# Counting sort of a GNN kernel: counts on two engines, one scan for the first columns, reload in two parts

## The chip, the cores and the metric

The kernel runs on one core of a Trainium2 chip. The metric is the device time of one execution in microseconds (us). "Before" is the kernel as it stood, "after" the kernel with the change below. Engines are called by their names in the profile: PE (TensorE), DVE (VectorE), ACT (ScalarE), POOL (GpSimd), SP (SyncE).

## What is computed

Four graph networks in a row work on 3125 nodes of 128 features and 50,000 edges. Each needs gathers by source node and sums by destination node. The first of them is, in short:

```python
h = jnp.maximum(_layernorm(x), 0.0)                   # 3125 x 128
h = relu(_bn(h @ fc_w + fc_b))
for i in range(2):
    d = segment_sum(ones, col)                        # degrees
    val = edge_weight * rsqrt(d[col]) * rsqrt(d[row])
    z = segment_sum(val[:, None] * h[row], col) @ conv_w[i] + conv_b[i]
    h = relu(_bn(z)) + h
x = x + h
```

The three others (an attention over `leaky(h_src, h_tgt, edge features)`, a dot-product attention with 8 heads, and two gated sums) go over the same edges. Per edge, `edge_attr @ W_edge @ a` is wanted too (4 scores).

## The kernel before

**Stages.** The nodes are split into NB = 25 blocks of 128. The edges are first sorted by destination block, so that each tile of 128 edges belongs to one block; there are TILES = 416 tiles with padding, in GROUPS = 52 groups of G = 8 tiles. Then six passes run over the tiles (`PASSES`), one for each layer. In each of them POOL issues one indirect DMA for each tile (L568, 416 a pass), which gathers 128 rows of a table in DRAM; DVE builds one-hot matrices, PE sums by them. Between two passes the node features go through PE, ACT and DVE, and SP stores the next table (`tab_dram[k]`, L498 and L500).

**The sort.** The edges lie as 125 lanes by COLS = 400 columns. SP loads `e_dst`, `e_src`, `e_w` (L470 to L472, semaphore `s_load_e`), then `wedge`, the small `abd` columns, the first two parts of the edge features (`ea`), `x`, and writes the initial records `recS` to `rec_dram` (L487, semaphore `s_recinit`). DVE makes constants (L1240 to L1252), fills `recS` and `rec_all` (L1254 to L1260), works out the block `e_blk` of each edge (L1265, L1266), local numbers, the record's fields (L1268 to L1273), counts for each lane and each of the 25 blocks how many edges lie in it (L1279, `tot`), and waits for two matmuls on PE (`prefixes`, L958) that turn the counts into bases. PE reaches `prefixes` in its edge-feature loop when i is 2 (L996). Eight small instructions (L1286 to L1293) make `base_pos`. `place(0, FIRST, ...)` then gives the first 80 columns their places: for each of 25 blocks a comparison (L1302), a scan (L1305) and a predicated copy (L1310), and five instructions that turn places into row numbers (L1315 to L1319). `place(FIRST, COLS, ...)` does the other 320.

**Scatter and reload.** POOL waits for the initial records (`s_recinit`) and for the first places (`s_placed`), then writes the records of one column after the other with 400 indirect DMAs (L545); group g of 8 columns also waits for the edge scores of ACT (`s_esc`). It needs the second `s_placed` at column 80. When all have landed, SP loads the sorted records back into `recU` (L491), and after that it stores the table of pass 0, which has been ready for long. DVE copies the source numbers out of `recU` (L1628), and POOL's first gather waits for that and for the stored table. While POOL gathers, DVE clears `ACC` (L1633), makes the first one-hots (L1624) and splits the records into three bf16 parts (`split`, L1520 to L1523).

**Order.** Each engine runs its instructions in order of the program. `link` waits for the instruction before it, `queued` does not. SP's and ACT's DMAs are issued in order of their programs too. Nothing is planned by a scheduler.

Of the kernel before, what the change touches and what calls it, by code (L numbers as in the profile page):

```python
# [8 lines left out]
ALU = mybir.AluOpType  # L9
ACT = mybir.ActivationFunctionType  # L10
AX = mybir.AxisListType.X

P = 128
# [8 lines left out]
FIRST = 80  # L22
TILES = (E // P + NB + 15) // 16 * 16
# [107 lines left out]
def gnn_kernel(nc, x, src, dst, edge_attr, edge_weight, fc_w, fc_b, conv_w, conv_b, bn_gamma, bn_beta,  # L131
               W_node, W_edge, a_vec, Wq, bq, Wk, bk, Wv, bv, Wo, bo, Wt, bt, Wg, bg, out):
    ctx = ExitStack()
    with ctx:
# [13 lines left out]
        lane_i = sb("lane_i", [P, 1], I32)  # L148
        iota = sb("iota", [P, 512])
# [132 lines left out]
        ranks = OH[0:LANES, :, :, :].rearrange("p a t f -> p (a t f)")[:, 0:5 * COLS].rearrange("p (c e) -> p c e", e=COLS)  # L282
        newblk = sb("newblk", [P, 2, SLOTS * H + 1])
# [17 lines left out]
        s_tot = sem("s_tot")  # L301
        s_pre = sem("s_pre")
# [166 lines left out]
        def _(sp):  # L469
# [16 lines left out]
            sp.wait_ge(s_recdef, 1)  # L486
            sp.dma_start(rec_rows, recS[:, :, :].rearrange("p t r -> p (t r)")).then_inc(s_recinit, 16)  # L487

            for r in range(3):
                sp.wait_ge(s_scat[r], 16 * G * ((COLS // G - 1 - r) // 3 + 1))  # L490
            sp.dma_start(recU.rearrange("p t r -> p (t r)"), rec_rows).then_inc(s_recl, 16)  # L491
# [11 lines left out]
            for k in range(len(PASSES)):  # L503
# [70 lines left out]
        def _(act):  # L574
# [6 lines left out]
            for k, v in enumerate([fc_b, conv_b[0], conv_b[1], bn_gamma[0], bn_gamma[1], bn_gamma[2],  # L581
                                   bn_beta[0], bn_beta[1], bn_beta[2]]):
                act.dma_start(cols[:, k:k + 1], v.rearrange("(p o) -> p o", o=1)).then_inc(s_load_w, 16)
            for k, v in enumerate([bo, bt[0], bt[1], Wg[0], Wg[1]]):
                act.dma_start(cols[:, 9 + k:10 + k], v.rearrange("(p o) -> p o", o=1)).then_inc(s_load_w, 16)
            for k, v in enumerate([bq, bk, bv]):
                act.dma_start(bqkv[:, k, :], v.rearrange("(o f) -> o f", o=1).broadcast_to([P, D])).then_inc(s_load_w, 16)
            act.dma_start(bgb[:, :], bg.rearrange("(o f) -> o f", o=1).broadcast_to([P, 2])).then_inc(s_load_w, 16)
# [50 lines left out]
            def only(chunk, work):  # L639

                return lambda c, n: work() if c == chunk else None

# [215 lines left out]
        def _(pe):  # L858
# [109 lines left out]
            pe.wait_ge(s_ue, 1)  # L968

# [19 lines left out]
            for i, buf, loads in edge_loads(pe):  # L989
# [6 lines left out]
                if isinstance(i, int) and i == 2:  # L996
                    prefixes()
# [217 lines left out]
        def _(dve):  # L1215
# [24 lines left out]
            link(v.tensor_copy(iota[:, :], iota_i[:, :]))  # L1240
            link(v.tensor_copy(lane[:, :], lane_i[:, :]))
# [5 lines left out]
            link(v.memset(sg16[:, :, :, :], 0.0))  # L1247
            link(v.memset(zero, 0.0))
            link(v.memset(onesb[:, :], 1.0))
            link(v.memset(c128b[:, :], float(P)))  # L1250
            link(v.tensor_scalar(lane_diag[:, :, :], ident[:, :].unsqueeze(1).to_broadcast([P, 4, P]), lane[:, 0:1], None, ALU.mult))
            link(v.tensor_scalar(iota2[:, :], iota[:, 0:P], 2.0, -float(P - 1), ALU.mult, ALU.add))  # L1252
            dve.sem_inc(s_consts, 1)
            link(v.memset(recS[:, :, :], 0.0))  # L1254
            link(v.memset(recS[:, :, R_DST], float(P)))
            dve.sem_inc(s_recdef, 1)


            dve.wait_ge(s_load_e, 48)
            link(v.memset(rec_all[:, :, :], 0.0))  # L1260
            link(v.tensor_scalar(spare[:, :], lane[:, :], float(COLS), float(P * TILES - LANES * COLS), ALU.mult, ALU.add))
            link(v.tensor_scalar(row_all[:, :], iota[:, 0:COLS], spare[:, 0:1], None, ALU.add))
            dve.sem_inc(s_recbase, 1)
            for ends, blk, loc in ((e_dst, e_blk[:, :], rec[:, :, R_DST]), (e_src, e_sblk[:, :], e_sloc[:, :])):
                link(v.tensor_single_scalar(e_int[:, :], ends[:, :], 7, ALU.arith_shift_right))  # L1265
                link(v.tensor_copy(blk, e_int[:, :]))  # L1266
                link(v.tensor_copy(e_rank[:, :], ends[:, :]))
                link(v.scalar_tensor_tensor(loc, blk, -float(P), e_rank[:, :], ALU.mult, ALU.add))  # L1268
            link(v.tensor_copy(rec[:, :, R_SRC], e_rank[:, :]))
# [4 lines left out]

            scratch = [e_rank[:, :], e_pos[:, :]]
            with dve.Fori(0, NB // 5, 1) as b5:
                for c in range(5):
                    b = 5 * b5 + c
                    v.tensor_scalar(scratch[c % 2], e_blk[:, :], iota[0:LANES, bass.ds(b, 1)], 0.0, ALU.is_equal, ALU.add,  # L1279
                                    accum_out=tot[:, bass.ds(b, 1)]).then_inc(s_tot, 1)  # L1280
                    if c:
                        dve.wait_ge(s_tot, b)
                dve.wait_ge(s_tot, 5 * b5 + 5)
# [10 lines left out]
            link(v.memset(e_pos[:, :], 0.0))  # L1294
            link(v.memset(e_w[:, :], 0.0))

            def place(c0, c1, ranked, carry):

                step = 16 if carry else 15
                with dve.Fori(0, NB // 5, 1) as b5:  # L1300
                    for c in range(5):
                        v.tensor_scalar(inside[:, c, c0:c1], e_blk[:, c0:c1], iota[0:LANES, bass.ds(5 * b5 + c, 1)], None, ALU.is_equal).then_inc(s_rank, 1)  # L1302
                    for c in range(5):
                        dve.wait_ge(s_rank, ranked + step * b5 + c + 1)
                        v.tensor_tensor_scan(ranks[:, c, c0:c1], e_w[:, c0:c1], inside[:, c, c0:c1], base_pos[:, bass.ds(5 * b5 + c, 1)],  # L1305
                                             ALU.add, ALU.add).then_inc(s_rank, 1)
                    for c in range(5):
                        dve.wait_ge(s_rank, ranked + step * b5 + 10 + c)
                        dve.sem_inc(s_gate, 1)
                        v.copy_predicated(e_pos[:, c0:c1], inside[:, c, c0:c1], ranks[:, c, c0:c1]).then_inc(s_rank, 1)  # L1310
                    if carry:
                        v.tensor_copy(base_pos[:, bass.ds(5 * b5, 5)], ranks[:, :, c1 - 1]).then_inc(s_rank, 1)
                    dve.wait_ge(s_rank, ranked + step * b5 + step)
# [7 lines left out]

            place(0, FIRST, 0, True)
            place(FIRST, COLS, 16 * NB // 5, False)

# [289 lines left out]
            def sum_pass(k, weighted):  # L1614
# [11 lines left out]

                dve.wait_ge(s_recl, 16)
                link(v.tensor_copy(idx_u[:, :], recU[:, :, R_SRC]))  # L1628
# [380 lines left out]
```

## Time and profile before

| what | value |
|---|---|
| time, median of 3 runs | 4109.13 us (4102.37 to 4113.22) |
| the profiled execution: its time | 4107.58 us |
| the profiled execution: its span in the trace | 4105.7 us |
| POOL busy | 2773.8 us, 2902 instructions |
| DVE busy | 1833.0 us |
| PE busy | 1935.3 us |
| ACT busy | 1079.0 us |
| first scatter starts, last starts | 73.23 us, 585.78 us |
| first gather starts | 601.03 us |

The span is what the trace covers; the execution's time is 1.9 us longer. A row of a timeline gives the start, the duration, the engine, the line, what is written and read, and in brackets how long the engine was idle before and what released it. DMA_INDIRECT on POOL is the work of making the descriptors of one indirect DMA, not the transfer.

### The profile page before, as it was taken

The page shows a single profiled execution, that of the slowest core. Times are in us where ns is not written, and L with a number is a line of the kernel's source. Part 1 is how long each engine was busy: PE and PEld are TensorE (multiplying, and loading weights), DVE is VectorE, ACT ScalarE, POOL GpSimd, SP SyncE. Part 2 cuts the span into 40 slices and gives each one's busy share as a digit, 9 for nine tenths or more (in the row PEclk, how much of TensorE's full clock was granted, in tenths as well). Part 3 has the DMA queues.
Part 4 walks back from the last instruction along what each step waited for, and adds up shares of the span by engine and source line. Part 5 has one row for each costly group of instructions (what it writes and reads, how often), then busy time and mean ns, then how long its engine had stood idle before and what let it go on. Part 6 is the DMA issues. An engine that isn't in the chain of part 4 may idle for free. (4 is left out here: it accounts for less than half of the span.)

```text
span 4105.7 us, 45490 instructions
## 1 busy us (share of the span) xinstructions
PE 1935.3 (47%) x10431; PEld 1712.0 (42%) x10432; DVE 1833.0 (45%) x4489; ACT 1079.0 (26%) x3099; POOL 2773.8 (68%) x2902
## 2 busy tenths in 40 slices
PE   7622005666644333467676455655543333433332
PEld 6611004555533333356676344555433333333332
DVE  7891016777643222335656647887721110211111
ACT  2101002222210000157777357777410000000000
POOL 2777767777747777467777167777257777577775
PEclk9996556666665555655556578787765565665565
DMA  4100012122222222233333244444212222321223
GB/s 126 51 4 4 3 37 53 52 52 52 51 47 53 52 52 53 29 97 80 80 80 75 18 144 130 130 133 125 35 54 53 52 52 52 51 53 52 52 52 55
DMA packets 147115, 254.60 MB, mean 62 GB/s; under 512 B 58948, under 2 KB 82915, under 8 KB 146712
## 3 DMA queue, kind: packets, MB, share of 16 engines
q0 software_dynamic: 99328, 193.52, 20.6%
q1 hardware_dynamic: 40618, 46.93, 3.9%
q10 hardware_dynamic: 7022, 12.64, 0.9%
q14 instruction: 109, 0.89, 0.1%
q8 instruction: 38, 0.62, 0.1%
HBM read 236.59 MB, written 16.30 MB: 62 GB/s over the span
## 5 line engine op out<-in xcount | busy, mean ns | idle before, releaser
L568 POOL DMA_INDIRECT arena<-tab_dram,tblk x832 | 794.0, 954 | 415.3 <-issue 253.0
L568 POOL DMA_INDIRECT pool<-tab_dram,tblk x816 | 776.3, 951 | 422.5 <-issue 247.9
L1100 PE MATMUL psum<-pool 128*128 128x128 f32 x1344 | 313.5, 427 | 556.5 <-DMA pool<-tab_dram,tblk 556.5
L1100 PEld LDWEIGHTS psum<-pool 128*128 128x128 f32 x1344 | 290.6, 328 | 580.8 <-issue 580.8
L545 POOL DMA_INDIRECT rec_dram<-arena,ACC x400 | 392.0, 980 | 193.3 <-issue 121.2
L568 POOL DMA_INDIRECT ACC<-tab_dram,tblk x432 | 408.5, 946 | 131.7 <-issue 131.7
L568 POOL DMA_INDIRECT pool<-tab_dram,arena x416 | 402.2, 967 | 140.8 <-issue 126.5
L1077 PE MATMUL psum<-pool 128*128 128x128 f32 x832 | 193.0, 426 | 477.4 <-DMA pool<-tab_dram,arena 393.3
L1077 PEld LDWEIGHTS psum<-pool 128*128 128x128 f32 x832 | 180.0, 328 | 481.4 <-issue 296.8
L1155 PE MATMUL psum<-pool 128*128 128x136 f32 (+1 forms) x1664 | 325.5, 369 | 43.4 <-DVE pool L1748 39.2
L1155 PEld LDWEIGHTS psum<-pool 128*128 128x128 f32 x1664 | 302.2, 265 | 55.1 <-issue 31.4
L687 ACT ACTIVATE arena<-psum,key 128x128 bf16<-128x128 f32 x416 | 146.3, 377 | 648.3 <-PE psum L1020 648.3
L1824 DVE TENSOR_TENSOR ACC<-ACC,pool 128x132 f32 (+1 forms) x832 | 242.9, 292 | 40.7 <-issue 6.1
L1589 DVE TENSOR_TENSOR pool<-psum,recS 128x1024 f32<-128x1024 f32 x56 | 68.0, 1223 | 421.7 <-PE psum L1100 421.4
L746 ACT ACTIVATE pool<-iota,recS 128x128 f32<-128x128 f32 x832 | 252.8, 387 | 0.0
L1100 PE MATMUL psum<-arena,ACC 128*128 128x128 f32 x576 | 134.3, 427 | 221.7 <-DMA ACC<-tab_dram,tblk 221.7
L1100 PEld LDWEIGHTS psum<-arena,ACC 128*128 128x128 f32 x576 | 124.8, 329 | 230.9 <-issue 230.9
L1589 DVE TENSOR_TENSOR arena<-psum,recS 128x1024 f32<-128x1024 f32 x48 | 58.2, 1222 | 351.0 <-PE psum L1100 351.0
L1131 PE MATMUL psum<-HN,pool 128*128 x832 | 161.4, 373 | 100.0 <-DVEq L1705 75.2
L1131 PEld LDWEIGHTS psum<-HN,pool 128*128 128x128 f32 x832 | 149.0, 277 | 113.0 <-issue 113.0
L1128 PEld LDWEIGHTS psum<-at,pool 128*128 128x128 f32 x832 | 165.4, 303 | 30.7 <-issue 30.7
L1128 PE MATMUL psum<-at,pool 128*128 x832 | 164.8, 330 | 23.5 <-ACT pool L724 15.6
(286 smaller groups left out, 3781.4 us busy)
## 6 DMA issues: line engine op xcount, KB each, us to landing
pool<-dst_dram SPq DMA_DIRECT2D x104, 256.0 KB, 3.5
arena<-tab_dram,tblk POOLq DMA_INDIRECT x832, 2.8
pool<-tab_dram,tblk POOLq DMA_INDIRECT x816, 2.5
HN<-in_edge_attr_dram ACTq DMA_DIRECT2D x23, 500.0 KB
ACC<-tab_dram,tblk POOLq DMA_INDIRECT x432, 2.5
pool<-tab_dram,arena POOLq DMA_INDIRECT x416
rec_dram<-arena,ACC POOLq DMA_INDIRECT x400, 2.1
tab_dram<-arena SPq DMA_DIRECT2D x24, 256.0 KB
```

The lines of the kernel that those rows point to most:

```text
L545: nc.gpsimd.indirect_dma_start(rec_dram, bass.IndirectOffsetOnAxis(ap=row_all[:, c:c + 1], axis=0), rec_all[:, c, :], None).then_inc(s_sca ...
L568: nc.gpsimd.indirect_dma_start(to[:, j, :], None, tab_dram[k], bass.IndirectOffsetOnAxis(ap=idx[:, G * g + j:G * g + j + 1], axis=0)).then ...
L687: nc.scalar.activation(signs[:, half, j, :], bank[j // 4][:, (j % 4) * P:(j % 4 + 1) * P], ACT.Sign, scale=-1.0, bias=key[:, bass.ds(G * g ...
L746: nc.scalar.activation(OHF[:, half, j, :], iota[:, 0:P], ACT.Square, scale=-1.0, bias=one[:, R_DST:R_DST + 1]).then_inc(s_osq, 1)
L1077: last = nc.tensor.matmul(bank[4 + 2 * (q % 2) + j // 4][:, (j % 4) * P:(j % 4 + 1) * P], rows[:, q, j, :], OH[:, q, j, :], start=True, st ...
L1100: last = nc.tensor.matmul(psum[:, bass.ds(vals[j] * P, P)], row if k in FLIPPED else one, one if k in FLIPPED else row, start=False, stop= ...
L1128: last_ = nc.tensor.matmul(bank[4 + half][:, 4 * j:4 * j + 4], OHT[:, half, j, :], at4[:, bass.ds(vals[j], 1), :].rearrange("p b h -> p (b ...
L1131: last_ = nc.tensor.matmul(bank[4 + j // 4][:, (j % 4) * P:(j % 4 + 1) * P], OHT[:, half, j, :], hn1[:, bass.ds(vals[j] * D, D)], start=Tr ...
L1155: last_ = nc.tensor.matmul(bank[j // 3][:, (j % 3) * ww:(j % 3 + 1) * ww], OHF[:, half, j, :], weighed[k][:, half, j, :], start=True, stop ...
L1589: v.tensor_tensor(OH8[slot], numbers.unsqueeze(1).to_broadcast([P, G, P]), recS[:, bass.ds(G * g, G), R_DST].unsqueeze(2).to_broadcast([P, ...
L1824: v.tensor_tensor(acc, acc, sums[k][:, which, tile, 0:sw], ALU.add).then_inc(s_sum, 1)
```

## The change

1. Constants: `recS` and `rec_all` are filled by POOL, not by DVE, right after its two iotas. POOL also fills `resets` (25 segments of 81: ones, and a zero at the head). Six constants that the counting doesn't need, and the four instructions on `e_src`'s block and local number, move behind the placement.
2. Counts: DVE counts the blocks 0 to 12 (LOWER = 13). ACT takes 12 sums of `Sign(mid - e_blk)`, which are cumulative counts; DVE turns their differences into the counts of the blocks 12 and up with two small instructions.
3. Prefixes: PE does them ahead of all edge features, behind its wait for `s_ue`, which ACT gives after its sums.
4. The record's fields are worked out by DVE behind its counts, while PE makes the prefixes.
5. The first 80 columns are placed by one comparison over 25 x 80, one scan over 25 x 81 that multiplies by `resets` and adds, one product and one reduction over the blocks.
6. SP: the initial records are written before `x` is loaded, with a wait until they have landed; the 18 small loads of `cols`, `bqkv` and `bgb` come from SP behind `x`, not from ACT. The table of pass 0 is stored before the wait for the scatter. The reload is two DMAs: the first EARLY = 64 tiles (`s_recf`), then the others (`s_recl`). POOL starts its gathers on the first, and waits for the second at group 8.

```diff
@@ sync
+            sp.wait_ge(s_recdef, 1)
+            sp.dma_start(rec_rows, recS[:, :, :].rearrange("p t r -> p (t r)")).then_inc(s_recinit, 16)
+            sp.wait_ge(s_recinit, 16)
             sp.wait_ge(s_consts, 1)
             sp.dma_start(X[:, 0:NB - 1, :], x[0:(NB - 1) * P, :].rearrange("(b p) f -> p b f", p=P)).then_inc(s_load_x, 16)
...
-            sp.dma_start(recU.rearrange("p t r -> p (t r)"), rec_rows).then_inc(s_recl, 16)
+            for c, n in T_CH:
+                sp.wait_ge(s_table, c + 1)
+                store(tab_dram[0], TABS[0], s_stored[0], c, n)
+            for r in range(3):
+                sp.wait_ge(s_scat[r], 16 * G * ((COLS // G - 1 - r) // 3 + 1))
+            sp.dma_start(recU[:, 0:EARLY, :].rearrange("p t r -> p (t r)"), rec_rows[:, 0:EARLY * REC]).then_inc(s_recf, 16)
+            sp.dma_start(recU[:, EARLY:TILES, :].rearrange("p t r -> p (t r)"), rec_rows[:, EARLY * REC:TILES * REC]).then_inc(s_recl, 16)
@@ gpsimd
+            nc.gpsimd.memset(rec_all[:, :, :], 0.0).then_inc(s_recbase, 1)
+            nc.gpsimd.memset(recS[:, :, :], 0.0).then_inc(s_recz, 1)
+            pool.wait_ge(s_recz, 1)
+            nc.gpsimd.memset(recS[:, :, R_DST], float(P)).then_inc(s_recdef, 1)
+            pool.wait_ge(s_iota, 3)
+            nc.gpsimd.memset(resets[:, :, 1:SEG], 1.0).then_inc(s_resets, 1)
+            nc.gpsimd.memset(resets[:, :, 0], 0.0).then_inc(s_resets, 1)
...
-            pool.wait_ge(s_recl, 16)
-                pool.wait_ge(s_idx, 1 if k == 0 else 2)
+                pool.wait_ge(s_idx, 1 if k == 0 else 3)
                 for g in range(GROUPS):
+                    if k == 0 and g == EARLY // G:
+                        pool.wait_ge(s_idx, 2)
@@ scalar
+            act.wait_ge(s_blk, 1)
+            for i in range(NB - LOWER):
+                if i >= 2:
+                    act.wait_ge(s_cum, i - 1)
+                nc.scalar.activation(signed[i % 2], e_blk[:, :], ACT.Sign, scale=-1.0, bias=mid[0:LANES, i:i + 1],
+                                     accum_out=cum[:, i:i + 1]).then_inc(s_cum, 1)
@@ tensor
-                pe.wait_ge(s_tot, NB)
+                pe.wait_ge(s_tot, LOWER + 1)
...
             pe.wait_ge(s_ue, 1)
+            prefixes()
...
-                if isinstance(i, int) and i == 2:
-                    prefixes()
@@ vector
+            link(v.tensor_single_scalar(e_int[:, :], e_dst[:, :], 7, ALU.arith_shift_right))
+            link(v.tensor_copy(e_blk[:, :], e_int[:, :]))
+            dve.sem_inc(s_blk, 1)
+            for b in range(LOWER):
+                v.tensor_scalar(scratch[b % 2], e_blk[:, :], iota[0:LANES, b:b + 1], 0.0, ALU.is_equal, ALU.add,
+                                accum_out=tot[:, b:b + 1]).then_inc(s_tot, 1)
...
+            link(v.tensor_tensor(tot[:, LOWER:NB], cum[:, 1:NB - LOWER + 1], cum[:, 0:NB - LOWER], ALU.subtract))
+            link(v.tensor_scalar(tot[:, LOWER:NB], tot[:, LOWER:NB], 0.5, None, ALU.mult))
+            dve.sem_inc(s_tot, 1)
+            dve.wait_ge(s_recbase, 1)
...
+            link(v.tensor_tensor(one_of[:, :, 1:SEG], e_blk[:, 0:FIRST].unsqueeze(1).to_broadcast([LANES, NB, FIRST]),
+                                 iota[0:LANES, 0:NB].unsqueeze(2).to_broadcast([LANES, NB, FIRST]), ALU.is_equal))
...
+            def place_first():
+                link(v.tensor_copy(one_of[:, :, 0], base_pos[:, :]))
+                dve.wait_ge(s_resets, 2)
+                link(v.tensor_tensor_scan(counted.rearrange("p b c -> p (b c)"), resets.rearrange("p b c -> p (b c)"),
+                                          one_of.rearrange("p b c -> p (b c)"), 0.0, ALU.mult, ALU.add))
+                link(v.tensor_tensor(chosen, one_of[:, :, 1:SEG], counted[:, :, 1:SEG], ALU.mult))
+                link(v.tensor_reduce(e_pos[:, 0:FIRST], chosen.rearrange("p b c -> p c b"), AX, ALU.add))
+                rows_of(0, FIRST)
+                link(v.tensor_copy(base_pos[:, :], counted[:, :, SEG - 1]))
...
+                dve.wait_ge(s_recf, 16)
+                link(v.tensor_copy(idx_u[:, 0:EARLY], recU[:, 0:EARLY, R_SRC]))
+                dve.sem_inc(s_idx, 1)
                 dve.wait_ge(s_recl, 16)
-                link(v.tensor_copy(idx_u[:, :], recU[:, :, R_SRC]))
+                link(v.tensor_copy(idx_u[:, EARLY:TILES], recU[:, EARLY:TILES, R_SRC]))
                 dve.sem_inc(s_idx, 1)
```

## Rows read from the trace of the kernel before

**Rows 1.** The gathers' line L568: durations in ns (min/median/max), then idle before it
```profile
L568 POOL DMA_INDIRECT pool<-tab_dram,arena x416: 940/947/5282, 601.0 to 1128.8; - x139
...
  issue: 759.1, 2490
  DMA tab_dram<-arena: 351.1, 6
```

**Rows 2.** Timeline of POOL: the scatter's first and last, the first gathers
```profile
73.23 1.14 POOL L545 DMA_INDIRECT rec_dram<-arena,ACC  x1 [71.74 <-DVEq L1320]
...
585.78 0.96 POOL L545 DMA_INDIRECT rec_dram<-arena,ACC  x1 [0.30 <-issue]
601.03 0.97 POOL L568 DMA_INDIRECT pool<-tab_dram,arena  x1 [14.29 <-DMA tab_dram<-arena]
...
606.07 5.28 POOL L568 DMA_INDIRECT pool<-tab_dram,arena  x1 [0.30 <-issue]
```

**Rows 3.** Timeline of DVE up to the first scatter
```profile
10.93 2.73 DVE L1260 MEMSET arena<- 128x3200 f32 x1 [0.84 <-DVE recS L1255]
...
14.45 0.37 DVE L1265 TENSOR_SCALAR pool<-pool 125x400 int32<-125x400 int32 x1
...
15.66 0.88 DVE L1268 SCALAR_TENSOR_TENSOR arena<-ACC 125x400 f32<-125x400 f32 x1
...
22.12 0.63 DVE L1279 TENSOR_SCALAR_CACHE_REDUCE ACC<-ACC,iota 125x400 f32<-125x400 f32 x1 [0.29 <-DVE arena L1273]
...
22.67 0.63 DVE L1279 TENSOR_SCALAR_CACHE_REDUCE ACC<-ACC,iota 125x400 f32<-125x400 f32 x1
...
44.14 0.19 DVE L1286 TENSOR_SCALAR tcount_i<-psum 128x25 int32<-128x25 f32 x1 [5.99 <-PE psum L962]
...
45.95 0.39 DVE L1294 MEMSET ACC<- 125x400 f32 x1
...
71.08 0.20 DVE L1315 CAST pool<-ACC 125x80 int32<-125x80 f32 x1 [0.21 <-DVE base_pos L1312]
...
72.07 0.24 DVE L1319 SCALAR_TENSOR_TENSOR ACC<-ACC 125x80 uint32<-125x80 f32 x1
```

**Rows 4.** Timeline of SP, POOL, PE: loads of the start, an iota, the prefixes
```profile
1.90 1.04 SPq L474 DMA_DIRECT2D wedge<-in_L_gnn_W_edge_dram  x2
...
0.85 0.55 POOL L533 IOTA pool<- 128x512 int32 x1 [0.40 <-POOLq L1999]
...
43.08 0.60 PE L961 MATMUL psum<-tot,tri 125*128 125x25 f32 x2
```

**Rows 5.** ACT: lines by form (the table load), then two neighbours of the sort's signs
```profile
L645 ACT ACT_TABLE_LOAD x1 | 1.3, 1283 | 17.5 <-issue 17.5
...
626.75 0.36 ACT L687 ACTIVATE arena<-psum,key 128x128 bf16<-128x128 f32 x1
...
627.10 0.36 ACT L687 ACTIVATE arena<-psum,key 128x128 bf16<-128x128 f32 x1
```

**Rows 6.** DVE, lines by form: scans of two lengths, a reduction
```profile
L1706 DVE TENSOR_REDUCE sg<-arena 128x64 f32<-128x1024 f32 x52 | 63.4, 1219 | 4.4 <-DVE arena L1693 3.0
...
L1305 DVE TENSOR_TENSOR_SCAN pool<-pool,base_pos 125x320 f32<-125x320 f32 x25 | 19.9, 857 | 0.0
...
L1305 DVE TENSOR_TENSOR_SCAN pool<-pool,base_pos 125x80 f32<-125x80 f32 x25 | 7.4, 361 | 0.0
```

**Rows 7.** DMA issues: KB each, median us from issue to landing; and SP's reload
```profile
rec_dram<-recS SPq DMA_DIRECT2D x1, 1664.0 KB, 17.8
arena<-rec_dram SPq DMA_DIRECT2D x1, 1664.0 KB, 7.6
...
587.93 0.35 SPq L491 DMA_DIRECT2D arena<-rec_dram  x1
```

**Rows 8.** Timeline, 1172 to 1178 us: a gather beside a memset on DVE
```profile
1172.52 4.71 POOL L568 DMA_INDIRECT pool<-tab_dram,tblk  x1 [42.80 <-DMA tab_dram<-arena]
1173.02 2.85 DVE L1545 MEMSET edgetab<- 128x3354 bf16 x1 [0.65 <-issue]
```

More of the change, by code:

```diff
@@ L22 @@
 FIRST = 80
+LOWER = 13
+EARLY = 64
 TILES = (E // P + NB + 15) // 16 * 16
@@ L301, in gnn_kernel @@
         s_tot = sem("s_tot")
+        s_blk = sem("s_blk")
+        s_cum = sem("s_cum")
+        s_recz = sem("s_recz")
+        s_resets = sem("s_resets")
+        s_recf = sem("s_recf")
         s_pre = sem("s_pre")
@@ L485, in _ @@
             sp.dma_start(X[0:TAIL, NB - 1, :], x[(NB - 1) * P:N, :]).then_inc(s_load_x, 16)
[L486 to L490, printed above, removed]
-            sp.dma_start(recU.rearrange("p t r -> p (t r)"), rec_rows).then_inc(s_recl, 16)
+            for k, v in enumerate([fc_b, conv_b[0], conv_b[1], bn_gamma[0], bn_gamma[1], bn_gamma[2],
+                                   bn_beta[0], bn_beta[1], bn_beta[2]]):
+                sp.dma_start(cols[:, k:k + 1], v.rearrange("(p o) -> p o", o=1)).then_inc(s_load_w, 16)
+            for k, v in enumerate([bo, bt[0], bt[1], Wg[0], Wg[1]]):
+                sp.dma_start(cols[:, 9 + k:10 + k], v.rearrange("(p o) -> p o", o=1)).then_inc(s_load_w, 16)
+            for k, v in enumerate([bq, bk, bv]):
+                sp.dma_start(bqkv[:, k, :], v.rearrange("(o f) -> o f", o=1).broadcast_to([P, D])).then_inc(s_load_w, 16)
+            sp.dma_start(bgb[:, :], bg.rearrange("(o f) -> o f", o=1).broadcast_to([P, 2])).then_inc(s_load_w, 16)
             TABS = {0: TAB[:, :, 0:D], 1: TAB[:, :, 0:D], 2: TAB[:, :, 0:D + 4],
@@ L1246, in _ @@
             link(v.memset(X[:, NB - 1, :], 0.0))
[L1247 to L1252, printed above, removed]
+            link(v.tensor_scalar(mid[:, :], iota[:, LOWER - 1:NB - 1], 0.5, None, ALU.add))
@@ L1253, in _ @@
+            link(v.memset(cum[:, NB - LOWER:NB - LOWER + 1], float(COLS)))
             dve.sem_inc(s_consts, 1)
-            link(v.memset(recS[:, :, :], 0.0))
-            link(v.memset(recS[:, :, R_DST], float(P)))
-            dve.sem_inc(s_recdef, 1)
             dve.wait_ge(s_load_e, 48)
-            link(v.memset(rec_all[:, :, :], 0.0))
-            link(v.tensor_scalar(spare[:, :], lane[:, :], float(COLS), float(P * TILES - LANES * COLS), ALU.mult, ALU.add))
-            link(v.tensor_scalar(row_all[:, :], iota[:, 0:COLS], spare[:, 0:1], None, ALU.add))
@@ L1263, in _ @@
[L1263 to L1269, printed above, removed]
+            link(v.tensor_single_scalar(e_int[:, :], e_dst[:, :], 7, ALU.arith_shift_right))
@@ L1273, in _ @@
             link(v.copy_predicated(rec[:, :, R_W], e_int[:, :], e_w[:, :]))
[L1275 to L1283, printed above, removed]
+            link(v.tensor_scalar(spare[:, :], lane[:, :], float(COLS), float(P * TILES - LANES * COLS), ALU.mult, ALU.add))
+            link(v.tensor_scalar(row_all[:, :], iota[:, 0:COLS], spare[:, 0:1], None, ALU.add))
             dve.wait_ge(s_pre, 1)
@@ L1293, in _, with rows_of @@
             link(v.tensor_tensor(base_pos[:, :], bank[6][0:LANES, 0:NB], tcount[0:LANES, 2, :], ALU.add))
[L1294 to L1313, printed above, removed]
+            def rows_of(c0, c1):
                 link(v.tensor_copy(e_int[:, c0:c1], e_pos[:, c0:c1]))
@@ new lines, in place @@
+            def place(c0, c1):
+                with dve.Fori(0, NB // 5, 1) as b5:
+                    for c in range(5):
+                        v.tensor_scalar(inside[:, c, c0:c1], e_blk[:, c0:c1], iota[0:LANES, bass.ds(5 * b5 + c, 1)], None, ALU.is_equal).then_inc(s_rank, 1)
+                    for c in range(5):
+                        dve.wait_ge(s_rank, 15 * b5 + c + 1)
+                        v.tensor_tensor_scan(ranks[:, c, c0:c1], e_w[:, c0:c1], inside[:, c, c0:c1], base_pos[:, bass.ds(5 * b5 + c, 1)],
+                                             ALU.add, ALU.add).then_inc(s_rank, 1)
+                    for c in range(5):
+                        dve.wait_ge(s_rank, 15 * b5 + 10 + c)
+                        dve.sem_inc(s_gate, 1)
+                        v.copy_predicated(e_pos[:, c0:c1], inside[:, c, c0:c1], ranks[:, c, c0:c1]).then_inc(s_rank, 1)
+                    dve.wait_ge(s_rank, 15 * b5 + 15)
+                rows_of(c0, c1)
@@ new lines, in _ @@
+            place_first()
+            link(v.memset(e_pos[:, FIRST:COLS], 0.0))
+            link(v.memset(e_w[:, FIRST:COLS], 0.0))
+            place(FIRST, COLS)
+            link(v.tensor_single_scalar(e_int[:, :], e_src[:, :], 7, ALU.arith_shift_right))
+            link(v.tensor_copy(e_sblk[:, :], e_int[:, :]))
+            link(v.tensor_copy(e_rank[:, :], e_src[:, :]))
+            link(v.scalar_tensor_tensor(e_sloc[:, :], e_sblk[:, :], -float(P), e_rank[:, :], ALU.mult, ALU.add))
+            link(v.memset(sg16[:, :, :, :], 0.0))
@@ L1325, in _ @@
+            link(v.memset(zero, 0.0))
+            link(v.memset(onesb[:, :], 1.0))
+            link(v.memset(c128b[:, :], float(P)))
+            link(v.tensor_scalar(lane_diag[:, :, :], ident[:, :].unsqueeze(1).to_broadcast([P, 4, P]), lane[:, 0:1], None, ALU.mult))
+            link(v.tensor_scalar(iota2[:, :], iota[:, 0:P], 2.0, -float(P - 1), ALU.mult, ALU.add))
             link(v.memset(tblk[:, :], 0.0))
```

29 lines of the change are left out of this document (18 added, 11 removed).

## The prediction

> **What bounds the kernel now.** I read POOL's waits first. At the line of the 2,496 gathers POOL waits for its own issue (about 0.30 us each time) and six times for a table between two stages, 351.1 us in all, and for nothing else [rows 1]; the scatter's line has one long wait, 71.74 us for DVE [rows 2]. POOL never waits for a ring slot, for an edge score or for the second placement. So POOL's program is one chain: start of the scatter, 400 scatters, a gap, then six passes of 416 gathers. An edit counts only if it moves the start (73.23 us), the gap between last scatter and first gather, or the pace of POOL. The timeline of POOL gives the two places [rows 2]: the start waits for DVE, the gap of 14.29 us is put down to the stored table. The timeline of DVE then shows what lies ahead of 73.23 us: DVE is nearly always busy, with constants, records, 25 counts, a wait of 5.99 us for PE, and the placement [rows 3].
>
> **Part 1: until `e_blk` is known.** DVE found the loads landed at its first look, about 10.1 us [rows 3]. They were on SP's queue ahead of `wedge`, whose two loads were issued by 2.9 us; the DMA view gives 3.5 us to landing for these, so I take 6.4 us for the end of the loads [rows 4] (upper end 10.1). Shift and cast follow at 0.40 us each from start to start (14.45 to 15.66 us is three such, [rows 3]): 7.2 us, 7.3 with the semaphore. DVE's own constants are over before that (the iota copy starts at 1.5 us, and what stays of them took 2 us).
>
> POOL now fills 3200 + 3328 + 416 + 2025 elements beside it. No memset of such a size on POOL is in the trace. The iota of 512 in 0.55 us [rows 4] gives 1.07 ns per element at most, 0.84 if 0.12 us of it is fixed. So the fills end at about 9 to 11 us. DVE and POOL get in each other's way: one gather on POOL took 4.71 us instead of 0.95 while DVE ran a memset of 2.85 us and a short copy behind it [rows 8], another 5.28 us beside the record split [rows 2]. No row shows the reverse. The price is then between 0 (no hold) and 4 us (shift and cast come after the last fill). I take 3, near the held end, since every row of the pair in conflict is one of a whole instruction. `e_blk` at 10.3 us.
>
> **Part 2: counts.** DVE: 13 x 0.55 us (22.12 to 22.67, [rows 3]) = 7.2 us, so 17.5. ACT: one table load of 1.28 us, then 12 signs. Its neighbours in the sort start 0.35 us apart at 128 columns [rows 5]; at 0.83 ns for each further column (500 against 32 columns of the edge features: 0.59 and 0.20 us) that is 0.57 us at 400, in all 1.28 + 12 x 0.57 = 8.1 us, 18.5 with the semaphore. ACT ends last, by 1 us. Two small DVE instructions (0.22 each) give 19.0 us. The same wait holds PE: `s_ue` comes behind ACT's signs, at about 18.5 + 0.4. The `abd` columns, on which PE waited until 14.3 us, are there by then. The matmuls take 1.06 us to DVE's next instruction (43.08 to 44.14 us, [rows 3, 4]): prefixes at 20.2 us.
>
> **Part 3: the record's fields**, in DVE's queue now before it reads the prefixes. Start to start: cast 0.40, local number 0.91, source 0.56, three for the weight 0.41 + 0.61 + 2.15, rows 0.76 (the kinds of the stretch of [rows 3]) = 5.8 us. The comparison over 2000 elements: 0.59 us at 415 elements and 3.63 at 3328 make 1.04 ns each, so 2.2 us. Sum 8.0: 27.0 us. The prefixes (20.2) are hidden under it, so the wait of 5.99 us is gone. If this cover were gone, it would cost 1.2 us. `s_recbase`, waited for at 19.0, comes at about 5 us.
>
> **Part 4: bases and placement.** Eight small instructions, 1.81 us (44.14 to 45.95, [rows 3]): 28.8. Then a copy 0.2; the scan: 361 ns at 80 and 857 at 320 elements [rows 6] are 2.07 ns each and 0.2 fixed, so 2025 take 4.4; product 2.2; reduction 1.22 us at 1024 [rows 6], at 1.04 ns for each further one 2.2; row numbers 1.23 (71.08 to 72.31, [rows 3]). With gaps 10.3: 39.1 us. POOL starts 0.92 us behind DVE's signal (72.31 to 73.23): **40.0 us, where it was 73.23: 33.2 us earlier.**
>
> What could be later than that: the initial records. `s_recdef` at about 8 to 9 us; SP is free at 9.4; issue and landing took 1.26 and 17.8 us behind `x` [rows 7]; now at most 28.5 us. Then SP waits with it, and `x` and the 18 small loads queue behind: `x` and weights are wanted first at 294 us. ACT loses those 18 issues (until 17.4 us), which is why it can count. Edge scores: PE started them at 19.75 us and gave one group in 2.5 us with a stop of 9 us for a load; they now start at about 20 and scatter groups take over 10 us. The second placement, 48.7 us as before, ends at 90 us; POOL comes to column 80 near 150.
>
> **Part 5: the scatter.** Same 400 instructions. Fourteen DVE instructions, about 4 us, come to lie beside it. In the first 49 us of the scatter 35 indirect DMAs took 1.39 us each instead of 1.264, beside 43 us of DVE work, so 0.1 us per us: +0.4; by the 0.5 us that one long instruction cost, up to 2. I take **+1.0**.
>
> **Part 6: the gap.** SP issued the reload 1.19 us after the last scatter's end (586.74 to 587.93, [rows 2, 7]). 1664 KB landed in 7.6 us. The first part is 256 KB: between 3.4 (the 64 KB loads) and 7.6; the last piece of the table, 26.5 KB behind six of 256, was there 3.7 us after its issue, so 4.0. The copy of the indices 0.3 with its wake, POOL 0.92. Gap 6.4 us instead of 14.29: **-7.9**. The table, stored since 300 us, no longer ends it. The second part is there by 9 us after the last scatter; POOL wants it 80 us later.
>
> DVE's memset of `ACC`, 2.89 us, ran from 597.66 while POOL was idle. Now it runs from about 11 us after the last scatter, and POOL gathers from 6.4 on. By [rows 8] it holds POOL: between 0 and 3.8 us, I take its length, **+2.9**. The split's hold [rows 2] stays as it is: some more gathers before it, the same instructions in it. The Trainium skill, page "SBUF — State Buffer", section "Who interferes with whom", says for trn2 that a DVE instruction with at most one SBUF input outside the 2-port modes doesn't contend with GpSimd; by this the memset would cost nothing. Rows 8 speak against it, or for the short copy behind it.
>
> **Sum.** -33.2 - 7.9 + 2.9 + 1.0 = -37.2 us. From the profiled run: 4107.58 - 37.2 = 4070.4; from the median of the runs: 4071.9. The profiled run lies 1.5 us below the median, within a spread of 11. I say 4071. All six stages behind keep their chain: POOL's pace 1.25 us, and the waits of 351.1 us less this gap.
>
> **Rivals.**
> (a) The memset holds nothing. The rest as above: 4071 - 2.9 = 4068. For it: only one row of such a hold, and a copy is in it. Against: that copy was 0.63 us long. The page's rule just named gives this case. Chance 0.22.
> (b) POOL's fills are slow, and the initial records end the wait. At r ns per element they are ready at 1.5 + 6.94 r us, landed 19.1 later; from r = 2.8, 2.6 times the iota's rate, this passes 40.0. At r = 4: 48.4, +8.4, so 4079. For it: no large fill on POOL in the trace. Against: the iota, and the 17.8 us had `x` ahead of it. Chance 0.11.
> (c) It doesn't do what it says: the reduction reads with a step of 320 bytes, the comparison and product with broadcasts, and all three run far below one element per 1.04 ns. At six times the price each, 3 x 11 = +33: 4104, no change that can be told. Against: the copy out of the records, with a step of 32 bytes, took 0.53 us for 416. Chance 0.02.
> (d) Slower: POOL's pace. A gather is 0.947 + 0.30 us, a scatter 0.96 + 0.30 [rows 1, 2]. POOL's program changes in its layout and its waits. If each of the 2,496 gathers took 1.270 instead of 1.250 (the scatter's pace and a little), +50 us: 4121. From 1.2655 on the change makes it slower. Against: the gathers of all passes have the same median of 947 ns. Chance 0.03.
>
> **How the numbers follow.** Forecast 0.62, (a) 0.22, (b) 0.11, (c) 0.02, (d) 0.03. Low end: port 0 (-3.0), memset 0 (-2.9), landing 3.4 (-0.6), scatter (-0.6) are 4064, and the runs' own spread adds 4 to that: 4060. High end: (b) and 4 for the spread: 4083. A change of 0.3%, 12.3 us, is about what a measurement of this kernel can tell. Faster: forecast, (a), (b), less a little for what I haven't thought of, 0.94; same 0.03; slower 0.03.
>
> **What the profile of after would show.** First scatter at 37 to 41 us; the last DVE count and the last sign within 1.5 us of each other; no wait of DVE for the prefixes; POOL's fills of 2.7 to 3.6 us each, and early DVE constants stretched beside them; a scan of 4.4 us; a gap of 6 to 7 us before the first gather; a gather of some 3.8 us a few gathers in. The prediction is wrong if the start is held by `s_recinit`, if a stage between passes gets longer, or if POOL's median gather isn't 947 ns.

## The result, and the profile after

After runs in 4066.7 us (median of 4, 4065.1 to 4074.08); before, on the same chip, in 4109.63 us (median of 4). The ratio is 0.9898, 95% interval 0.9886 to 0.9909: 43 us less, where 37 had been forecast (4071 us, range 4060 to 4083). The profiled execution has a span of 4063.3 us, 42.4 us less than before.

The timeline of POOL shows the fills, the scatter's start and the first gathers; they answer to [rows 2].

```profile
1.44 2.75 POOL L563 MEMSET arena<- 128x3200 f32 x1
4.14 2.86 POOL L564 MEMSET recS<- 128x3328 f32 x1
7.06 1.01 POOL L566 MEMSET recS<- 128x416 f32 x1
7.92 1.82 POOL L568 MEMSET pool<- 125x2000 f32 x1
...
42.28 1.15 POOL L580 DMA_INDIRECT rec_dram<-arena,ACC  x1 [32.38 <-DVEq L1331]
...
553.97 0.96 POOL L580 DMA_INDIRECT rec_dram<-arena,ACC  x1 [0.30 <-issue]
560.21 0.97 POOL L603 DMA_INDIRECT pool<-tab_dram,arena  x1 [5.28 <-DVEq L1680]
...
566.49 0.94 POOL L603 DMA_INDIRECT pool<-tab_dram,arena  x1 [0.30 <-issue]
...
574.00 4.59 POOL L603 DMA_INDIRECT pool<-tab_dram,arena  x1 [0.30 <-issue]
```

The scatter starts at 42.28 us, not 73.23; the gap is 5.28 us, not 14.29. Its releaser is now the signal of DVE (L1680) behind its copy of the source numbers out of the first part of the reload. Since POOL's indirect DMAs are one chain, the whole span can be cut at its starts and ends:

| stretch (us) | before | after | difference |
|---|---|---|---|
| until the first scatter | 73.23 | 42.28 | -30.95 |
| 400 scatters | 513.51 | 512.65 | -0.86 |
| gap to the first gather | 14.29 | 5.28 | -9.01 |
| pass 0, 416 gathers | 528.69 | 527.11 | -1.58 |
| passes 1 to 5 together | 2611.45 | 2606.72 | -4.73 |
| the five waits between passes | 336.82 | 341.23 | +4.41 |
| behind the last gather | 27.75 | 28.02 | +0.27 |

So 40 us are the two places that the prediction named. Of the rest, 6 were won inside the passes, where POOL's median gather takes 944 ns instead of 947, and 4 were lost between passes; neither was forecast.

DVE until the scatter, to be read beside [rows 3]:

```profile
1.52 5.77 DVE L1273 CAST iota<-pool 128x512 f32<-128x512 int32 x1 [0.63 <-POOL lane_i L561]
...
7.63 2.19 DVE L1276 TENSOR_SCALAR ident<-iota,lane 128x128 f32<-128x128 f32 x1
...
11.68 0.37 DVE L1287 CAST ACC<-pool 125x400 f32<-125x400 int32 x1
...
19.73 0.17 DVE L1297 TENSOR_TENSOR tot<-cum 125x12 f32<-125x12 f32 x1 [0.27 <-ACT arena L674]
...
20.25 0.37 DVE L1302 CAST ACC<-pool 125x400 f32<-125x400 int32 x1
...
28.00 0.18 DVE L1315 TENSOR_SCALAR tcount_i<-psum 128x25 int32<-128x25 f32 x1
...
29.92 4.38 DVE L1337 TENSOR_TENSOR_SCAN pool<-pool 125x2025 f32<-125x2025 f32 x1
34.33 2.24 DVE L1339 TENSOR_TENSOR pool<-pool 125x2000 f32<-125x2000 f32 x1
36.61 3.49 DVE L1340 TENSOR_REDUCE ACC<-pool 125x80 f32<-125x2000 f32 x1
```

The iota copy takes 5.77 us instead of 0.43: it ends at 7.29 us, just behind POOL's second fill (7.00). DVE waits 0.27 us for ACT's last sign and not at all for the prefixes. There is a surprise in the last row: the reduction takes 3.49 us.

The 31 us of the start can be laid on the stages by the two timelines of DVE. `e_blk` is ready 3.2 us earlier (12.05 for 15.23). From there to the first instruction on the bases it is 16.0 us instead of 28.9, through the counts on two engines, the work on `e_src` moved away, and the hidden wait for PE. From the bases to the last row number of the first 80 columns it is 11.7 us instead of 26.4. Only the split of the counts was taken away alone in a run (`counts_on_dve`); the placement and the order of the fields were not.

### The profile page after: what moved, and what is told of

It is laid out like the page before. It is cut to its first block and busy times, and to the rows that moved or that the text cites. A ratio compares the mean times of both kernels' runs of the same rounds, so it can differ in the third digit from the quotient of the medians.

```text
span 4063.3 us, 45249 instructions
## 1 busy us (share of the span) xinstructions
PE 1921.5 (47%) x10431; PEld 1699.2 (42%) x10432; DVE 1821.7 (45%) x4393; ACT 1086.3 (27%) x3123; POOL 2775.2 (68%) x2907
## 5 line engine op out<-in xcount | busy, mean ns | idle before, releaser
L654 ACT ACTIVATE arena<-psum,cols 128x512 f32<-128x512 f32 (+1 forms) x42 | 26.5, 639 | 565.9 <-PE psum L920 565.6
L1707 DVE TENSOR_TENSOR ACC<-ACC,psum 128x128 f32 x416 | 119.4, 287 | 108.4 <-PE psum L1110 55.7
```

Source lines behind the costliest of these rows:

```text
L654: nc.scalar.activation(to, of, ACT.Identity, bias=bias).then_inc(s_zt, 1)
L1707: v.tensor_tensor(acc, acc, bank[4 + 2 * (q % 2) + j // 4][:, (j % 4) * P:(j % 4 + 1) * P], ALU.add).then_inc(s_acc, 1)
```

## The experiments

Every kernel but `before_again` is after with the edit shown. "Start" is the start of the first scatter.

**The kernel before, a second trace.** No edit.

> The kernel before once more, for its trace on this chip. In the first pair of traces a gather took 947 ns before and 944 ns after (median), which over 2,496 gathers makes 6 us of the 42; five of the six waits between passes differed by 1 to 5 us, with both signs (+4.4 in all). Theory: the waits between passes vary from run to run and are no effect of the change; then this trace shows them 1 to 5 us off the first one. Whether the 3 ns belong to the kernel or to the chip or the run is open: with 947 again they belong to the kernel, with 944 to the run.

Start 73.07 us, gap 14.38, 947 ns for a gather again (last pass 519.98 us). The five waits made 338.9 us, against 336.8 in the first trace of the same program. So waits between passes do differ by a few us with no change at all.

**POOL's fills behind `e_blk`.**

```diff
+            pool.wait_ge(s_blk, 1)
             nc.gpsimd.memset(rec_all[:, :, :], 0.0).then_inc(s_recbase, 1)
```

> After, with POOL's fills behind a wait for e_blk (s_blk). Theory: POOL's two large fills hold the port that DVE's iota copy (5.77 us instead of 0.43) and ident (2.19 instead of 0.29) want, and this delays e_blk to 12.05 us. Then these two take 0.43 and 0.29 us, e_blk is there when the loads are (7.3 to 8 us), and the first scatter starts at 37.5 to 38.5 us instead of 42.28: 4 us less in all. Rival 1: something else stretches the iota copy (its table in SBUF, a cold start); it stays at 5.8 us and the start at 42. Rival 2: the initial records now land last (their fill ends at about 14 us, 14.7 us to landing and 1 for POOL): the start is then not before 30 us, no effect; if landing takes 24 us as the time from issue of a load behind it, the start stays near 39 to 40.

```profile
1.53 0.43 DVE L1274 CAST iota<-pool 128x512 f32<-128x512 int32 x1 [0.63 <-POOL lane_i L561]
...
2.29 0.28 DVE L1277 TENSOR_SCALAR ident<-iota,lane 128x128 f32<-128x128 f32 x1
...
9.48 0.37 DVE L1287 TENSOR_SCALAR pool<-pool 125x400 int32<-125x400 int32 x1 [5.59 <-DMA pool<-in_edge_weight_dram]
```

That is DVE's timeline. The hold is shown: with the fills away the two instructions take 0.43 and 0.28 us, not 5.77 and 2.19. But `e_blk` comes at 10.25 us, not 7.3 to 8, because the loads land at 9.4: my expectation for them was wrong. Start 40.71 us, 1.6 earlier than after, where 4 had been expected. The initial records, written at 16.88 us, landed before 24.3 (SP's next issue) and held nothing. The time, 4068.7 us (ratio to before 0.9888, 0.9869 to 0.9906), isn't told apart from after's (0.9898, 0.9886 to 0.9909); gathers took 947 ns in this trace.

**The ten weight loads from SP behind `x`** (and the fills behind `e_blk`).

```diff
-            for k, w in enumerate([W_node, Wq, Wk, Wv, Wo, Wt[0], Wt[1]]):
-                act.dma_start(wraw[:, k, :], w).then_inc(s_load_w, 16)
...
+                sp.dma_start(wraw[:, k, :], w).then_inc(s_load_w, 16)
```

> fills_later, with the ten weight loads of ACT (640 KB) moved to SP behind x. In fills_later DVE is free at 3.9 us and waits for the edges' numbers until 9.48 us. Theory: the ten loads share the DMA engines with them; without them 590 KB are there by 6.0 to 7.5 us, the first scatter starts 2 to 3.5 us earlier than fills_later's 40.71, at 37.2 to 38.7. Rival: the loads are bound by their own latency and descriptors on SP's queue; still 9.4 and 40.7. The weights are wanted at 250 us, so nothing else moves.

```profile
7.69 0.37 DVE L1287 TENSOR_SCALAR pool<-pool 125x400 int32<-125x400 int32 x1 [3.80 <-DMA pool<-in_edge_weight_dram]
```

In DVE's timeline the loads are there at 7.7 us instead of 9.5; start 38.94. `fills_again` and `together`, the same two starts once more, have the loads at 9.03 and 7.95 us and the start at 40.35 and 39.25. So the other 640 KB cost 1.1 to 1.8 us. Median 4069.1 us over runs from 4058.4 to 4072.3, ratio 0.9896 (0.9869 to 0.9923): no difference from after that the times can tell.

**One reload, the table still stored early.**

```diff
+            sp.dma_start(recU.rearrange("p t r -> p (t r)"), rec_rows).then_inc(s_recl, 16)
-            sp.dma_start(recU[:, 0:EARLY, :].rearrange("p t r -> p (t r)"), rec_rows[:, 0:EARLY * REC]).then_inc(s_recf, 16)
-            sp.dma_start(recU[:, EARLY:TILES, :].rearrange("p t r -> p (t r)"), rec_rows[:, EARLY * REC:TILES * REC]).then_inc(s_recl, 16)
```

> After, with the reload in one DMA again, and the table still stored before the scatter's end. Theory: the gap of 14.29 us before was ended by the table's store, and its move alone gives a good part: gap 1.2 + 6.6 (landing of 1664 KB with no stores beside) + 0.6 + 1.0 = 9.4 us, so of the 9.0 us won in the gap 4.9 come from the order of the store and 4.1 from the two parts. Rival: the reload itself took 7.6 us and ended the gap; then the gap is 11 or more.

```profile
555.44 0.33 SPq L528 DMA_DIRECT2D arena<-rec_dram  x1
...
562.32 0.53 DVE L1678 CAST arena<-arena 128x416 uint32<-128x416 f32 x1 [257.04 <-DMA arena<-rec_dram]
...
563.70 0.97 POOL L602 DMA_INDIRECT pool<-tab_dram,arena  x1 [9.48 <-DVEq L1680]
```

These are rows of SP, DVE and POOL. The gap is 9.48 us (9.4 expected): the order of the table's store is worth 4.8 of the 9.0 us, the two parts 4.2. The other traces with two parts have gaps of 4.9 to 5.0 us, so the parts are worth 4.2 to 4.6.

**All 25 counts on DVE.**

```diff
-            for b in range(LOWER):
+            for b in range(NB):
...
-            act.wait_ge(s_blk, 1)
-            for i in range(NB - LOWER):
```

> After, with all 25 counts on DVE and none on ACT. Theory: DVE's 25 counts take 13.75 us from e_blk (12.05 us) and end at 26.0 instead of 20.1, so the record's fields, which follow, end at 33.8 and the first scatter starts 5.5 to 6 us later, at 48 us; PE's prefixes stay hidden under the fields. Rival: something else of the start (the initial records, the bases) hides part of it; the start moves by under 4 us.

Start 48.22 us, 5.9 later, as expected. Nothing else of the start hides a part of it.

**The product stored by column.**

```diff
-        chosen = ....rearrange("p (b c) -> p b c", c=FIRST)
+        chosen = ....rearrange("p (c b) -> p c b", b=NB)
```

> After, with the product (chosen) stored with the blocks innermost, so that the reduction reads neighbouring elements and the product writes with a step of 25 elements. Theory: the reduction took 3.49 us instead of 2.2 since it reads with a step of 320 bytes; now 2.2 to 2.3 us, the product stays at 2.24, and the first scatter starts at 41.0 us instead of 42.28. Rival 1: the step costs the same on writing; the product takes 3.5 us and nothing is won. Rival 2: the reduction is slow for another reason (groups of 25 are short); it stays at 3.5 us.

```profile
34.33 3.85 DVE L1339 TENSOR_TENSOR pool<-pool 125x2000 f32<-125x2000 f32 x1
38.21 2.24 DVE L1340 TENSOR_REDUCE ACC<-pool 125x80 f32<-125x2000 f32 x1
```

The reduction is now 2.24 us, as at one element in 1.04 ns, with its groups of 25 as they were: the step was its price. But the product, which now writes with a step, took 3.85 instead of 2.24. Start 42.63 us, nothing won: rival 1.

The trace of before already had this price. The local numbers of the destination go to the record with a step of 32 bytes, in 0.88 us [rows 3]; the same instruction for the source writes without a step:

```profile
17.79 0.57 DVE L1268 SCALAR_TENSOR_TENSOR ACC<-ACC 125x400 f32<-125x400 f32 x1
```

Its step cost 0.31 us for 400 elements, or 0.8 ns each. The product's step cost 0.8 ns each too, and the reduction's, on the read side, 0.6.

**The record split in pieces.**

```diff
-                link(v.tensor_copy(parts[0], x))
+                pieces = [slice(TILES * i, TILES * (i + 1)) for i in range(REC)]
+                for s in pieces:
+                    queued(v.tensor_copy(parts[0][:, s], x[:, s]))
+                dve.wait_ge(s_dve, done[0])
...
```

> After, with each of the four instructions that split the records cut into 8 pieces of 416 elements. They hold three gathers for 2.22, 4.59 and 4.06 us instead of 0.94: 8.0 us. Theory: the port is held for one instruction and POOL gets its turn between two; then no gather beside the pieces takes over 1.8 us, the excess is 2 to 4 us, and the kernel is 4 to 6 us faster, though DVE has 28 instructions more (3 us). Rival: DVE, whose pieces follow without a gap, keeps the port; then one or two gathers take 8 us or more and the kernel is 0 to 3 us slower.

The first fence is after, DVE and then POOL; the second is this run.

```profile
570.88 2.01 DVE L1571 CAST pool<-arena 128x3328 bf16<-128x3328 f32 x1
572.93 3.63 DVE L1572 TENSOR_TENSOR arena<-arena,pool 128x3328 f32<-128x3328 f32 x1
576.59 1.89 DVE L1573 CAST arena<-arena 128x3328 bf16<-128x3328 f32 x1
578.51 3.63 DVE L1574 TENSOR_TENSOR pool<-arena 128x3328 bf16<-128x3328 f32 x1
...
571.48 2.22 POOL L603 DMA_INDIRECT pool<-tab_dram,arena  x1 [0.30 <-issue]
574.00 4.59 POOL L603 DMA_INDIRECT pool<-tab_dram,arena  x1 [0.30 <-issue]
578.90 4.06 POOL L603 DMA_INDIRECT pool<-tab_dram,arena  x1 [0.30 <-issue]
```

```profile
569.93 2.56 DVE L1573 CAST pool<-arena 128x416 bf16<-128x416 f32 x8
572.53 4.11 DVE L1576 TENSOR_TENSOR arena<-arena,pool 128x416 f32<-128x416 f32 x8
...
569.29 1.43 POOL L603 DMA_INDIRECT pool<-tab_dram,arena  x1 [0.30 <-issue]
571.02 0.99 POOL L603 DMA_INDIRECT pool<-tab_dram,arena  x1 [0.30 <-issue]
572.32 0.99 POOL L603 DMA_INDIRECT pool<-tab_dram,arena  x1 [0.30 <-issue]
573.61 1.33 POOL L603 DMA_INDIRECT pool<-tab_dram,arena  x1 [0.30 <-issue]
```

No gather takes over 1.43 us; ten of them are held for 2.4 us together, where three were held for 8.0. DVE needs 13.6 us instead of 11.3. Pass 0 takes 521.33 us instead of 527.11. POOL gets its turn between the pieces. That isn't so everywhere: in after the gather at 574.00 starts inside one long instruction (to 576.56) and ends 0.1 us behind the next (578.48). So a hold isn't bounded by one DVE instruction. The medians are 4062.6 (ratio to before 0.9882, 0.9866 to 0.9899) and 4066.7; the intervals overlap, so the 5.8 us are shown by the trace alone.

**The copy behind the edge table's memset, later.** The line moves from `edge_start` to `edge_lasts`:

```diff
-                link(v.tensor_copy(spread.rearrange("p (t h) -> p t h", h=H), ident[:, :].unsqueeze(2).to_broadcast([P, P, H])))
```

> After, with the copy of ident into spread (0.63 us) moved from behind the memset of the edge table (bf16, 3354 elements, 2.85 us) to the third group of that pass. The pass's first gather took 4.54 us beside the two, while the memset of ACC (f32, 3400 elements, 2.89 us) held no gather in pass 0. Theory: the bf16 memset holds the port, and the copy only adds its own 0.6; the gather now takes 3.3 to 4.0 us. Rival: only the copy holds it, asked for by DVE ahead; the gather takes under 1.5 us. The kernel's time moves by less than 3 us.

```profile
1129.70 4.07 POOL L603 DMA_INDIRECT pool<-tab_dram,tblk  x1 [43.29 <-DMA tab_dram<-arena]
1130.03 2.85 DVE L1596 MEMSET edgetab<- 128x3354 bf16 x1 [0.65 <-issue]
1132.80 1.95 DVE L1637 TENSOR_SCALAR pool<-iota,recS 128x128 f32<-128x128 f32 x8
```

4.07 us, a little over the 3.3 to 4.0 expected: without the copy the gather ends 0.9 us behind the memset (1133.77 against 1132.88). So the hold of [rows 8] doesn't need the copy; it lasts through the memset.

**The same memset as f32 words.**

```diff
-                queued(v.memset(etab[:, :, :], -BIG))
+                queued(v.memset(edgetab[:, 0:PAIRS * (P + 1) // 2], TWO_BIG))
```

> After, with the edge table's memset (bf16, 3354 elements, 2.85 us) written as f32 words of the same bytes, 1677 elements. It held the first gather of pass 1 for 4.5 us, where the memset of ACC (f32) held none. Theory: a memset in f32 doesn't hold POOL; it takes 1.45 us, and the gather beside it under 2 us (what the copy of 0.63 us behind it holds). Rival: any memset that lies in the second half of a gather holds it, and the one of ACC was lucky; then the gather takes 2.5 to 3.3 us.

```profile
1131.91 2.84 POOL L604 DMA_INDIRECT pool<-tab_dram,tblk  x1 [42.75 <-DMA tab_dram<-arena]
1131.93 1.46 DVE L1597 MEMSET edgetab<- 128x1677 f32 x1 [0.30 <-issue]
1133.30 0.63 DVE L1598 COPY pool<-ident 128x1024 f32<-128x1024 f32 x1
```

The memset takes half the time, and the gather 2.84 us instead of 4.54. But a gather that wasn't held would have been over at 1132.85, before the copy starts; this one ends 0.8 us behind the copy. So it was held during the f32 memset too: my theory that the type decides is wrong. The rival named 2.5 to 3.3 us, and the time is in that range, but its reason (that `ACC`'s memset was lucky) isn't the answer either: three gathers ran at 0.94 us beside that one, and none beside it took over 0.98 in any trace of a kernel with the change.

That the held gather is mostly the first of its pass isn't the reason, as `counts_on_dve` shows:

```profile
1137.01 0.94 POOL L603 DMA_INDIRECT pool<-tab_dram,tblk  x1 [43.80 <-DMA tab_dram<-arena]
1137.75 2.85 DVE L1585 MEMSET edgetab<- 128x3354 bf16 x1 [0.65 <-issue]
1138.26 3.70 POOL L603 DMA_INDIRECT pool<-tab_dram,tblk  x1 [0.31 <-issue]
1140.52 0.63 DVE L1586 COPY pool<-ident 128x1024 f32<-128x1024 f32 x1
```

There the first gather was nearly over when the memset began and wasn't held; the second was. What tells the two memsets apart stays open. One difference in the program was varied by no run: `ACC`'s memset is a `link`, so DVE waits for its end before it goes on, and the edge table's is `queued`, with the copy (in `copy_later` the one-hots) right behind it. So it isn't shown whether the memset itself holds POOL or the instruction queued behind it does.

**One more wait on POOL.**

```diff
+            pool.wait_ge(s_iota, 2)
             nc.gpsimd.memset(rec_all[:, :, :], 0.0).then_inc(s_recbase, 1)
```

> After, with one more wait on POOL ahead of its fills, for a semaphore that is long there (s_iota at 2), so that nothing is delayed. The pace of the gathers (median 947 ns in both traces of before and in fills_later, 944 in after, one_reload and split_sliced; 520.0 against 518.9 us for the last pass) follows the kernel, on the same chip. Theory: it is where POOL's instructions come to lie; fills_later has one instruction more than after ahead of everything. Then this kernel has 947 ns and 520.0 us too. Rival: it is the work or the time at which the fills run; then 944 ns and 518.9 us stay.

944 ns and 518.96 us in the last pass: a further instruction on POOL, by itself, isn't the cause of the two paces.

**The fills behind `e_blk`, a second trace** (on another chip).

> fills_later once more, for a second trace of the same program. Its gathers took 947 ns (median) and its last pass 520.0 us, while weights_late, with the same program on POOL, took 944 ns and 519.0, and one_more_wait, with the same number of instructions there, too. Theory now: the 3 ns belong to the execution and not to the program; then this trace can have either, and 944 here settles it. Rival: they belong to the program; then 947 and 520.0 again.

947 ns and 519.98 us again. In the two programs that have two traces the pace repeats: 947 ns in before and in `fills_later`, both times. Of the programs with one trace, `edge_f32` has 947 ns; after and eight others have 944. What of the program sets it is open. It isn't POOL's instructions alone: `weights_late` has those of `fills_later`, and 944 ns.

**Together:** fills behind `e_blk`, weights from SP, the split in pieces, the edge table in f32.

> weights_late (fills behind e_blk, weights on SP), the record split in 8 pieces, and the edge table's memset written as 1677 words of f32 with the same bytes. Theory, from the traces so far: the first scatter starts at 38.9 us (weights_late) instead of 42.28, the split holds POOL for 2.4 us instead of 8.0, the edge table's memset for at most 1.7 instead of 3.6; in all 3.4 + 5.7 + 1.9 = 11 us less than after, 4056 us. Rival: what POOL wins in pass 0 and 1 is given back in the wait that follows, since DVE ends its part of the pass later; then 4060 or more.

4059.65 us, where 4056 had been expected; ratio to before 0.9877 (0.9861 to 0.9894), where after has 0.9898 (0.9886 to 0.9909). The median is the best of all, but the intervals overlap, so the times don't show that it beats after. In the trace, whose execution was the fastest of the four (4052.96), start 39.25 us (-3.0 against after), pass 0 520.47 (-6.6), pass 1 521.83 (-1.7); the wait behind pass 0 is 43.99 us, after had 44.03, so nothing is given back there.

## Why the prediction was right, step by step

**The bound** was read rightly: both places moved the end by their full size, 40.0 of the 42.4 us.

**Part 1, `e_blk`:** 12.1 us, 10.3 said. Two terms failed. The loads were there at 9.4 us and not at 6.4; that SP's queue serves loads in order was my reading, and the landing of small loads behind them was no measure. And the hold by POOL's fills was in the place that I didn't price: not at the shift but at the constants, which I had called over by then. That `e_blk` came out only 1.8 us later than said hides two misses, 3.1 us at the loads and the wrong place of a hold priced at 3. The fills took 0.86 ns per element, inside the 0.84 to 1.07 that the iota gave. Here the Trainium skill, page "SBUF — State Buffer", section "Who interferes with whom", says that whichever of GpSimd and a 2-port DVE instruction issues first has the port for its whole instruction; if the iota copy is such an instruction, the trace goes further: it started beside the first fill (to 4.19) and ended 0.3 us behind the second (to 7.00), so it wasn't served between them. `fills_later` and `fills_again` show what the hold is worth here, 1.6 and 1.9 us, since the loads are late anyway.

**Part 2, counts:** 8.2 us from `e_blk` to the next instruction, 8.7 said. The table load ran at 5.79 us, ahead of the wait, not behind it (-1.3); a sign took 0.61 us and not 0.57 (+0.5). `counts_on_dve` gives the worth of the split, 5.9 us.

**Part 3, fields:** 7.75 us, 8.0 said; the prefixes were hidden.

**Part 4, bases and placement:** 13.4 us until the last row number at 41.36, 12.1 said. Bases 1.7, scan 4.38, product 2.24 as worked out; the reduction 3.49 instead of 2.2. The mechanism was rival (c)'s, at 1.6 times the price and not six, and for this instruction alone. I had held against it that the copy out of the records, with a step of 32 bytes, took 0.53 us for 416 elements. That was no sign of a free step: casts of 400 without one take 0.37 us. Start 42.28 instead of 40.0. The initial records landed before 24.1 us.

**Part 5, scatter:** -0.9 us instead of +1.0. In `fills_later`, with the pace of before, it is 513.70 against 513.51. By this the moved instructions cost 0.2 us, and the faster pace of after's program gives back 1.

**Part 6, gap:** 5.28 us, 6.4 said. The first part landed 3.0 us from its issue, not 4.0. The memset of `ACC` held nothing: +2.9 was wrong, rival (a) right. I had taken [rows 8] for a rule; it is true of what happens there (`copy_later`) and not of this memset. The rule of the Trainium skill that the prediction names from the page "SBUF — State Buffer", section "Who interferes with whom" (no contention for at most one input outside the 2-port modes), agrees with the trace for `ACC`'s memset. Beside the edge table's memset gathers were held, and whether that is against the rule depends on the open question above.

**Not in the sum:** the time inside the passes, -6.3 us, most of it POOL's pace (944 for 947 ns), and the waits between passes, +4.4. Rival (d) had the pace as a danger; it moved by a seventh of that, the other way. The waits sum to 337 to 348 us over all traces. The last one varies most, 34.5 to 45.3 us, and goes with the granted clock of TensorE. Here it is in before and in `one_reload` (columns: stretch, its length, busy PE, PEld, DVE, ACT, POOL, mean granted clock as a share of full speed, DMA share, GB/s):

```profile
3523.60:3558.07 34.47, 21.72 (x118) 15.61 (x119) 20.35 (x39) 9.63 (x21) 0.00 (x0) 0.70 0.33 55
```

```profile
3482.50:3527.80 45.30, 32.73 (x119) 23.79 (x119) 20.88 (x39) 9.87 (x21) 0.06 (x2) 0.55 0.25 41
```

PE does the same work in 21.7 and 32.7 us at 0.70 and 0.55, DVE and ACT are alike. That is 11 us of noise from one wait: `one_more_wait`, whose edit delays nothing, has 45.3 us there too, where after has 39.2.

**The sum.** The pair of traces is 42.4 us apart, and 37.2 were said. Four terms were better than said: the memset (2.9 us), the gap (1.1), the scatter (1.9) and the passes (6.3). Three were worse: the start (2.3), the waits (4.4) and the end behind the last gather (0.3). The size of the two main terms was earned: 40.0 us measured, 41.1 said. That the whole came within 6 us is partly luck, since 12.2 us of misses in one direction met 7.0 in the other, and two of the largest weren't in the sum at all.

**The signs it named.** Two of the three signs of being wrong did come: the median gather is 944 ns and not 947, and the waits between passes got longer. Neither touches the two places, and the second is within what those waits vary by. The start (42.28) lies outside the 37 to 41 us that the profile was to show, the gap (5.28) outside 6 to 7, and the gather of 3.8 us a few gathers in is missing. The fills of 2.75 and 2.86 us, the stretched constants, the scan of 4.38 us and the counts and signs that end 0.1 us apart are as said.

## What to carry to other kernels

Where one engine's queue is the whole chain, cut the span at its long waits first, before and after; every edit is worth what it moves in that table. A fill that is moved from DVE to an idle POOL isn't free: put it behind the instructions that DVE needs first. Cut long DVE instructions beside a descriptor-making POOL into pieces. Before a load is called landed, look for a row in which someone waits for it. An instruction's price with a step is read from a row that has one.

## What the hardware showed that wasn't expected

- DVE's iota copy started beside POOL's first fill and ended only behind the second (5.77 us for 0.43). In the other direction POOL got its turn between DVE's queued pieces (no gather over 1.43 us), but one gather was held across two long instructions (4.59 us).
- A step of 320 bytes on the read side makes 2000 elements cost 3.49 instead of 2.24 us, a step of 100 bytes on the write side 3.85. A step of 32 bytes on the write side makes 400 elements cost 0.88 us instead of 0.57.
- Beside one memset (3400 elements, DVE waits for its end) no gather of POOL was held. Beside another (3354 elements in bf16 or 1677 in f32, with the next instruction queued behind it) a gather was held to its end or longer.
- The same indirect DMAs took 944 or 947 ns (median of 2,496) depending on the program; two programs were traced twice and kept their pace.
